# GNN and mixture-of-experts kernel on one Trainium2 core: other waits in front of the eight row gathers of an oct

## What is computed

```
enh = layernorm(x) + 0.1 * query_emb          # 3125 nodes x 256
Q, K, V = enh @ Wq + bq, enh @ Wk + bk, enh @ Wv + bv     # 4 heads of 64
mod_k  = K[src] + 0.2 * rel_w[edge_type]
scores = sum_d(Q[dst] * mod_k) / 8
w      = softmax of scores over the edges of one dst
agg    = segment_sum(w * V[src], dst)
x = x + layernorm(agg @ Wo + bo + ...) * gamma + beta
x = x + MoE(layernorm(x))                     # 16 experts, 2 per token
```

## Time and profile before

| | |
|---|---|
| median of 3 runs | 1333.86 us (1328.99 to 1337.06) |
| the profiled execution, device time | 1346.19 us |
| its span, first to last instruction | 1344.4 us |
| granted TensorE clock over the span | 0.868 of full |
| gathers (L632) | 440, busy 421.0 us on GpSimd |

### The profile page before, as it was taken

How to read it: one execution, slowest core, us unless ns; L and a number is a source line. 1 busy time by engine, 2 the same in 40 slices (tenths; PEclk the granted TensorE clock), 3 DMA queues, 4 the chain that set the end, 5 groups by cost and what they waited for, 6 DMA issues and landing times.

```text
span 1344.4 us, 23897 instructions
## 1 busy us (share of the span) xinstructions
PE 1080.3 (80%) x7032; PEld 851.6 (63%) x7033; DVE 894.0 (66%) x1856; ACT 666.2 (50%) x2365; POOL 716.4 (53%) x714
## 2 busy tenths in 40 slices
PE   8978567776767777676677777799599999999997
PEld 3445345555545555555555565567389999999996
DVE  4767767677777877777777768889944444444443
ACT  5532356667667776576676766557511111111111
POOL 4455555555555655555556554756055555445663
PEclk9997777778888978777878878897699999999999
DMA  6266666656766666567666665602744444655332
GB/s 211 94 180 189 195 196 192 202 183 178 221 189 206 193 194 204 179 202 210 198 199 198 174 208 142 202 5 92 256 119 118 100 100 95 184 150 130 53 52 28
DMA packets 112993, 215.77 MB, mean 160 GB/s; under 512 B 19403, under 2 KB 57211, under 8 KB 112891
## 3 DMA queue, kind: packets, MB, share of 16 engines
q0 software_dynamic: 47488, 132.68, 36.7%
q1 hardware_dynamic: 59973, 80.16, 18.4%
q10 hardware_dynamic: 5430, 1.73, 0.6%
HBM read 191.96 MB, written 22.54 MB: 160 GB/s over the span
## 4 chain that ended last, share of the span: by engine, by line
PE 49%; DVE 21%; issue 16%; another core or an unknown queue 9%; ACT 2%; DMA 1%; DVEq 1%; SPq 0%; POOL 0%; POOLq 0%
PE qe_ps L1920 13%; PE bank L1929 8%; PE qe_ps L1732 6%; DVE ring L881 6%; PE bank L1772 5%; PE bank L1920 4%; DVE acc L893 3%; PE qe_ps L1772 2%; DVE ring L875 2%; DVE score L887 2%; PE qe_ps L1837 1%; PE qe_ps L1650 1%; PE qe_ps L1909 1%; PE bank L1650 1%
## 5 line engine op out<-in xcount | busy, mean ns | idle before, releaser
L632 POOL DMA_INDIRECT ring<-kv_table,src_idx x440 | 421.0, 957 | 330.4 <-DVE ring L881 181.5
L1502 ACT ACTIVATE wv<-ring,wgt 128x64 f32<-128x64 f32 x1628 | 407.3, 338 | 52.9 <-remote 46.5
L1732 PE MATMUL qe_ps<-q,hot_t 128*128 x1320 | 237.1, 316 | 140.0 <-issue 87.6
L1732 PEld LDWEIGHTS qe_ps<-q,hot_t 128*128 128x128 bf16 x1320 | 134.6, 110 | 209.0 <-issue 179.3
L1772 PE MATMUL bank<-wv,hotf 128*128 128x260 f32 x588 | 188.6, 451 | 25.2 <-issue 18.8
L697 POOL DMA_INDIRECT out<-room,slot_i x64 | 119.2, 1863 | 154.9 <-DMA out<-room,slot_i 81.4
L1920 PEld LDWEIGHTS qe_ps<-xg_t,ring 128*128 128x128 f32 x1536 | 181.4, 192 | 4.9 <-issue 1.7
L1621 ACT ACTIVATE act<-qe_ps 128x512 f32<-128x512 f32 x64 | 38.2, 597 | 294.7 <-PE bank L1920 140.9
L875 DVE TENSOR_TENSOR ring<-ring,bank 128x1024 f32<-128x1024 f32 x110 | 133.3, 1212 | 75.8 <-remote 63.3
L1920 PE MATMUL qe_ps<-xg_t,ring 128*128 128x128 f32 x1536 | 182.0, 275 | 1.3 <-issue 0.7
L881 DVE TENSOR_TENSOR ring<-ring,qe_ps 128x512 f32<-128x512 f32 x220 | 148.8, 677 | 26.1 <-remote 18.2
(11 more groups left out here) (339 smaller groups left out, 1504.5 us busy)
## 6 DMA issues: line engine op xcount, KB each, us to landing
ring<-in_w SPq DMA_DIRECT2D x48, 512.0 KB, 7.1
t_row<-t_rows SPq DMA_DIRECT2D x55, 256.0 KB
d_row<-d_rows SPq DMA_DIRECT2D x55, 256.0 KB
ring<-kv_table,src_idx POOLq DMA_INDIRECT x440
kv_table<-ring SPq DMA_DIRECT2D x25, 256.0 KB, 2.0
out<-acc SPq DMA_DIRECT2D x26, 128.0 KB, 1.7
x_table<-ring SPq DMA_DIRECT2D x26, 128.0 KB, 1.9
ring<-in_x SPq DMA_DIRECT2D x12, 256.0 KB, 9.0
```

The costliest lines, as they stand in the source:

```text
L632: pool.indirect_dma_start(ring[:, u, place(g) * D:(place(g) + 2) * D], None, kv_table, bass.IndirectOffsetOnAxis(ap=src_idx[:, 4 * g + u:4 ...
L1502: ins = act.activation(wv[:, g % WV_N, u, h, 0:HD], v_rows(g)[:, u, h * HD:(h + 1) * HD], ACT.Copy, scale=w[:, col:col + 1])
L1732: ins = pe.matmul(q_ps[p % AHEAD][:, u * D:(u + 1) * D], hot_t[:, p // 4 % HB_N, hot_cols(p, u)], tile_of(q3, q_tiles[p % 4])[:, k * D:(k ...
```

## The change

Only the waits in front of the gathers change. In terms of the steps of VectorE:

| gather | before | after |
|---|---|---|
| `old` even (2o), u = 0 | reduce(2o) | the same |
| u = 1 | multiply(4o+2) | the same |
| u = 2 | multiply(4o+3) | the same |
| u = 3 | none | reduce(2o+1) |
| `old` odd (2o+1), u = 0 | reduce(2o+1) | the same |
| u = 1 | multiply(4o+4) | the same |
| u = 2 | multiply(4o+5) | add_relation(2o+3) |
| u = 3 | none | multiply(4o+5) |

```diff
             def gather(g):
-                a_red.wait(pool, g - DEPTH)
+                old = g - DEPTH
+                if old >= 0 and old % 2 == 0:
+                    due = ((a_red, old), (a_prod, 2 * old + 2), (a_prod, 2 * old + 3), (a_red, old + 1))
+                else:
+                    due = ((a_red, old), (a_prod, 2 * old + 2), (a_add, old + 2), (a_prod, 2 * old + 3))
                 b_wv.wait(pool, 2 * (g + DEPTH - PLACES) + 1)
                 for u in range(4):
-                    if u in (1, 2):
-                        a_prod.wait(pool, 2 * (g - DEPTH) + 1 + u if g >= DEPTH else -1)
+                    count, n = due[u]
+                    count.wait(pool, n if old >= 0 else -1)
                     pool.indirect_dma_start(ring[:, u, place(g) * D:(place(g) + 2) * D], None, kv_table,
                                             bass.IndirectOffsetOnAxis(ap=src_idx[:, 4 * g + u:4 * g + u + 1], axis=0)).then_inc(got[g % 4], 16)
```

## The result

On the chip of the first comparison the kernel after took 1349.84 us in the median of five runs (1348.44 to 1362.25), the kernel before 1328.99 us (1324.93 to 1337.06): **ratio 1.0144, interval 1.0087 to 1.0201**: slower on that chip, by more than the noise, though the interval reaches over 2%. (The medians alone give 1.0157. The 1333.86 us quoted ahead of the prediction is the median of the first three of the five runs of before.) Forecast was 1321 us, so the sign was wrong. The profiled execution of after took 1362.25 us (span 1360.5) against 1346.19 (span 1344.4) of before: 16 us more. Both are slower than their medians, by 12 and 17 us.

A forecast was written before the change was run, and what follows sets the result against it. No engine was full in the edge phase; TensorE was taken to stall while gathers issue back to back. 22 stalls, each 0.60 us shorter, take 13 us off 1333.9: 1321 us, own range 1309 to 1330, 8 in 10 1296 to 1356.

The forecast's parts named there:

- The timing of single gathers: Edge phase, GpSimd: odd quad's u = 2 starts 0.60 us earlier, even quad's u = 3 up to 0.28 us late.
- The delay is gone there: At the next gather but one, 0.60 us of idle time absorbs the even quad's 0.28 us delay.
- the part on the even quad: Its u = 3 now waits for reduce(2o+1), 0.28 us late; cost taken as 0, at most 3.5 us.
- The run ends at the same gather: Seven back-to-back gathers start 0.60 us earlier; the eighth still waits for the next oct's first multiply, behind the stall.
- 22 runs shorten their stall by 0.60 us: TensorE's stalls behind seven back-to-back gathers end earlier while their start stays: 13 us off in all.
- the pause was what mattered: Sign to look for in the changed profile: eight or ten back-to-back gathers instead of seven, and TensorE's idle time rising.
- the rival *Slower: The shortened idle time before odd u = 2 no longer lets TensorE catch up: 1366 us, 1350 for half; chance 0.27.
- Met waits cost 0: On GpSimd, a gather whose added wait is already met still follows its predecessor 0.30 us later, so costs nothing.
- The reading of the earlier trace: TensorE's query weight loads idled 165.9 us in 148 pieces for nothing the profile shows; this pointed to the stalls.
- while gathers are issued back to back TensorE's instructions reach it slowly: Edge phase: the supposed cause of TensorE's stalls, which end about 2.5 us after the last gather is issued.
- Weak in that the pattern may lock into another one: Caveat: a chunk's repeating pattern may settle differently, with a gain or loss larger than any forecast term.
- the last rival: Stalls beginning before reduce(2o+1) ends hold back gathers, freeing TensorE 2.5 us sooner: 55 us off, 1279 us; chance 0.08.

The follow-up runs named there:

- its two halves alone: Kernel before with only the odd quads' waits changed: ratio 1.0037; with only the even quads' waits changed: ratio 1.0051.
- the kernel two later: Kernel before; odd quads' u = 0 and 1 wait for multiply(4o+4), u = 2 for multiply(4o+5), even u = 3 for multiply(4o+4): 1364.51 us, 1.0101.
- The two kernels with later gathers: Kernel before with odd quads' gathers waiting one step later: 1378.07 us; the same with even quads' u = 3 waiting for multiply(4o+4) too: 1364.51 us.
- paced gathers: Kernel before with a GpSimd memset behind each gather from the fifth quad on, waited for by the next: 1253.19, 1248.76 and 1251.93 us.

## Why the prediction was wrong

**The timing of single gathers: right.** The odd quad's u = 2 went 0.60 us earlier and its pause fell to 0.52 us; the even quad's u = 3 went 0.28 us later.

**"The delay is gone there": this step of the part on the even quad failed.** I had priced the 0.28 us at 0, at most 3.5 us, because a pause of 0.60 us would take it up. Of this pause 0.30 us stand between any two gathers, so it had 0.30 to give and not 0.60. The delayed gather moreover fell on a comparison of VectorE (L869) and grew by another 0.28 us, and with both the pause was used up. Then the odd quad's earlier u = 2 made the second pause vanish instead of shrinking it to 0.52. I had worked out the two quads apart, each from the trace of before; together they close both pauses of one oct in four. The Trainium skill, "SBUF — State Buffer", "Who interferes with whom", says that a `tensor_scalar` of VectorE in a two-port mode and GpSimd shut one another out of a shared port. This trace agrees as far as times go: in the profiled execution of after, eleven gathers start 0.07 to 0.10 us behind the start of L869 and take 1.21 to 1.23 us, and ten start 0.05 to 0.07 us behind it and take 0.95. In which mode L869 ran, the trace doesn't say.

**"The run ends at the same gather" and 22 runs shorten their stall by 0.60 us: this is the step with the wrong sign.** Twelve runs of seven were left where 23 had been, and 18 runs of ten where there had been 9. Where the run of seven stayed, its stall did come out 0.6 us shorter in the median (3.5 instead of 4.1 us); where the run began three gathers sooner, it got 0.4 us longer (5.7 instead of 5.3). The total stood, 175 us against 174, where 13 us less was forecast. A chunk took 55.0 us in the mean of twelve, before 54.2, and not 1.1 us less. By my own text, runs of ten in place of seven meant that the pause was what mattered, and the rival *Slower* gave 1350 us for its half; measured were 1349.84. That agreement is chance as far as anything here shows, and I don't claim it: the rival needed stalls that grew by 16 us. Only 5.5 us of the profiled pair's 16 lie in the edge phase, and on chip 8 the same change gave 1.0006. There its edge phase ended at 879.4 us, in the first comparison at 885.5: the changed kernel differs between two executions by as much as before and after do there. The interval of the first comparison, 1.0087 to 1.0201, holds for that chip and that sitting; what made it 1.44% there stays open. The word "slower" is not refuted for that chip, and not shown for others: four comparisons give 1.0144, 1.0006, 1.0016 and 1.0012 for the change (its two halves alone 1.0037 and 1.0051).

**"Met waits cost 0": not refuted, nor shown to the last 0.5%.** 1.0037 with 106 more of them (1.0013 to 1.0060), where before against itself gives up to 1.0014 (0.9990 to 1.0039). That is 4 us, or some 40 ns for each, and 7 us at the end of the interval.

**The reading of the earlier trace rows: wrong as a size.** I took the 165.9 us of idle time for "issue" at L1732 as the stalls. The rows of the queries between 250 and 600 us, first with stalls (the profiled execution of before), then without (chip 1):

```profile
PEld qe_ps L1732 <- issue: 86.3, 77, 4.7
...
PE qe_ps L1732 <- issue: 43.5, 49, 2.1
```
```profile
PEld qe_ps L1732 <- issue: 84.4, 79, 3.3
...
PE qe_ps L1732 <- DVE ring L881: 59.5, 60, 2.9
```

The weight loads idle as long without a stall: a load stands behind a product that waits for VectorE, and the profile calls that "issue". What tells the two apart is the products' own idle time for "issue": 43.5 us with stalls, no such row without. The stalls' size came out nearly right all the same, 178 us by counting slow starts and 179 us by the edge phases of the two kinds of execution.

**What the waits of TensorE alone don't show: the other engines are held too.** In the same 350 us of the stalled execution there stand, among others,

```profile
ACT hotf L1496 <- remote: 53.2, 14, 7.1
...
DVE acc L893 <- remote: 43.3, 9, 7.5
```

All such rows come to 78.8 us on VectorE and 90.0 us on ScalarE, and chip 1 has none on either. So the stall doesn't seem to hold TensorE alone, which the prediction had in brackets only. What these two engines waited for, the rows don't say.

**The root, "while gathers are issued back to back TensorE's instructions reach it slowly": half right.** Where stalls occur, they go with runs: 35 of 38 runs of eight in the kernel two later, and an end 2.2 to 3.0 us behind the last gather in 116 of the 172 stalls of the five traces that have them (32 of 35 in the kernel two later). Against a simple length, one stall each of the change on chip 8 stands behind a run of two and a run of four gathers. And on three chips runs of 64 bring none. So a run is not enough; a second condition is needed that changes between chips (or with what else happens on them), and no run here shows it. The Trainium skill, "Runtime: NRT & Kernel Launch", "Instruction fetch mechanics", by which fetching is mostly hidden, agrees with the traces of chips 1, 13 and 14; where stalls occur something is not hidden for 5 us at a time. The trace holds the packets that load instructions. One of their two queues, the same row on the page of before and on that of chip 1:

```profile
q8 instruction: 45, 0.74, 0.2%
```

A packet of this queue takes 0.97 us in the median of the edge phase of before and 0.99 us on chip 1, the longest 1.7 and 1.4 us. And in 17 of the 35 stalls of before no instruction packet of either queue starts between 3 us ahead of the stall and 1 us behind it; that from 629.18 to 634.79 us is one. So slow packets of instructions are not what the stalls consist of. What holds back instructions that have been loaded was not tested. Nor does a stall need a lower clock: that from 643.0 to 647.9 ran at a granted clock of 1.00, the upper of the two levels.

**"Weak in that the pattern may lock into another one": this fits what came.** The changed program itself had 12 runs of seven and 18 of ten in the first comparison, 11 and 12 on chip 8. The two kernels with later gathers, which differ from each other by one wait, ended the edge phase 16 us apart on one chip, and 17 and 33 us later than the kernel after beside them.

**The ranges.** 1349.84 us lies between 1296 and 1356, the range given for 8 in 10, but that range held both signs and says little for the reasoning. Its lower end was called halfway to the last rival; half way from 1321 to 1279 us is 1300. Nothing hangs on it.

## What to carry to other kernels

Look first whether the time of the unchanged program holds on another chip: here it moved by 14 to 16%, nearly all of it in the one phase that was to be tuned, and the change under study was worth a tenth of that at most. Be slow to tune spacing waits to a stall of unknown cause: where stalls occur, three other orders of them gave ratios of 1.0006 to 1.0190 and never a gain, and where none occur, leaving them out cost 0.2 to 0.4%. What they are worth where stalls occur was not measured. When two edits each take a part of the same pause, work them out together, gather by gather, since the second starts from what the first has left; and count as the pause's room only what is above the gap that stands there anyway. And before a row of idle time is taken as a cost, find the same row where the cost is absent.

## What the runs showed of the hardware that I had not expected

- The same program took 1164.56 to 1166.05 us on three chips, 1352.45 us on chip 8 and 1328.99 us on the chip of the first comparison. Outside the edge phase the executions agree within 11 us; in it the stalled ones have 192 GB/s of transfers where the others have 249.
- TensorE had 440 gathers of 128 rows beside it, up to 95 in a row at 1.25 us, without one stall of the kind described, at a granted clock of 0.94 over the edge phase; with stalls that clock was 0.81. A stall doesn't need the lower clock: one of them ran at 1.00 throughout.
- The expert phase, which does not depend on the change, took 363 us in one execution and 374 in another of the same first comparison; on chip 8 it took 368, 367 and 363 us in three kernels. One and the same program, that with paced gathers, took 372 and 364 us for it in two executions on chip 1, so 8 of those 11 us need no change to come about.
- A gather's issue took 1.23 us instead of 0.95 when it started 0.08 us behind the start of VectorE's comparison of 128x1024 bf16, and 0.95 when it started 0.05 to 0.07 us behind it.
